# Scores of two items visited together in a one-core attention and expert block

## The chip, the cores and the metric

The kernel runs on one core of one Trainium2 chip. The metric is the device time of one execution in microseconds (us). TensorE is PE in the profile, its weight loads PEld, VectorE DVE, ScalarE ACT, GpSimd POOL, and SyncE (which issues the DMAs) SP.

## What is computed

For 16 batches of 512 rows with 256 channels: a layer norm, 16 heads of causal attention with RMS norm and rotary embedding on q and k, and beside it a layer of 8 experts of which each row takes one. Both are added to the input. Cut to what matters:

```python
xn = _layernorm(x)
q, k, v = split(einsum('btc,oc->bto', xn, wqkv))      # 16 heads of 64
q, k = rope(rmsnorm(q, q_norm_w)), rope(rmsnorm(k, k_norm_w))
attn = einsum('bhtd,bhsd->bhts', q, k) * D ** -0.5
attn = softmax(where(causal, attn, -inf))
out = einsum('bhts,bhsd->bhtd', attn, v) -> einsum('bte,ce->btc', out, wo)
chosen = argmax(einsum('bsh,eh->bse', xn, gate_w)); moe = xn + (xn @ expert_w[chosen])
return x + out + moe
```

## The kernel before

The work is cut into 128 units, one for each pair of heads of each batch (16 batches by 8 pairs). Rows come in four tiles of 128. `ITEMS = (1, 3, 2, 0)` is the order in which the row tiles of a unit are scored: item 0 is row tile 1 with 256 columns of keys, item 1 is tile 3 with 512, item 2 is tile 2 with 384 and item 3 is tile 0 with 128. Exact f32 products are made from high and low parts of the operands, in three terms (`TERMS`).

Every engine runs its own list of steps, written out by hand in a function `unit(u)`; the lists meet only at semaphores, and on each engine a step that waits holds all that stands behind it. While unit u is scored, unit u-1 is finished and units u+1 and u+2 are begun. The steps that matter here, with the name of the function, are:

- `qkv(u, t)` on PE: 6 products of 384 columns for row tile t. ACT takes the squares and v (`take_qkv`), DVE the products with cosine and sine and the sums (`rope_products`, three instructions), POOL adds and scales them. `transpose_qk` turns q and k, ACT and DVE split them in high and low part (`take_qk`).
- `scores(u, k)` on PE: for item k six products, three terms for each of two heads. A head has 64 rows of q and k, so a product uses half of the array's rows (64*128 in the profile) and the two heads' products start as a pair. Then two products over all rows add the causal mask on the diagonal tile (ident_b, mask_b, bf16). Items write two score buffers in turn, `ps_s[n % 2]`; the visit waits until the softmax two items back is done (`s_prob`).
- `row_max(u, k)` on DVE takes the maxima, `softmax(u, k)` on ACT the exponentials and their sums, two heads each.
- `transpose_probs(u, k)` (pt0 to pt3) turns the probabilities, ACT takes them (`take_pt`). One unit later `values(u)` multiplies them with v.
- `invert_sums(u)` on DVE: a reciprocal and a copy to row_inv. PE turns row_inv (`transpose_inverse`), ACT takes it (`take_inverse`), DVE multiplies (`normalise_o`), ACT and DVE split the result (`take_o`).
- `project(u)`: 12 products with w_out; DVE adds them (`take_projection`, to acc).
- `transpose_xs`, `expert` (xs, ex): one tile of sorted rows and its expert in most units.

Some units of a batch have extra steps on DVE: `row_stats` (pair 4), `normalise_x` (pair 5), `start_rows` (pair 1), `choose` (pair 7); every second batch `take_rank` (after `ranks` on PE), `find_slots` and `add_experts`. Units 0 to 7 have `split_weights`.

All PE outputs other than scores go to four general banks `ps_g` in strict rotation. `uses(u)` lists the uses of a unit in PE's order; a use waits for the release of the use four before it (`bank`). Reordering PE's list therefore also changes who has to have released what.

## Time and profile before

| | us |
|---|---|
| median of 3 executions | 2225.2 (2224.34 to 2225.23) |
| profiled execution | 2226.1 |
| its span, first to last instruction | 2224.0 |
| PE busy | 2119.9 (95%) |
| DVE busy | 1664.7 (75%) |
| ACT busy | 1526.2 (69%) |
| POOL busy | 1335.0 (60%) |
| granted TensorE clock, mean | 0.991 |

A busy engine is one that has an instruction of the program running; a wait is idle time before an instruction, put down to the semaphore that ended it. Matmuls overlap: what one costs is the distance between starts, not its duration. The profile's chain of work that ended last lies on PE for 78% of the span.

### The profile page before, as it was taken

What the parts mean: (1) busy time and instruction counts of PE and PEld (TensorE: products, weight loads), DVE (VectorE), ACT (ScalarE), POOL (GpSimd) and SP (SyncE); (2) the same over time, 40 slices, a digit from 0 to 9 for tenths busy, and PEclk for the clock granted to TensorE, in tenths of its full rate; (3) what the DMA queues carried; (4) which work ended last, traced back from release to release, by engine and by line L of the source; (5) the groups of instructions that cost most, each with busy time, mean ns of one, the idle gap of its engine ahead of it and who ended that gap; (6) DMA issues with size and microseconds to landing.
All of it is one profiled execution on the core that took longest, in us unless ns stands there. A gap on an engine that the chain in (4) does not pass through costs nothing.

```text
span 2224.0 us, 46872 instructions
## 1 busy us (share of the span) xinstructions
PE 2119.9 (95%) x16008; PEld 1685.9 (76%) x16008; DVE 1664.7 (75%) x3788; ACT 1526.2 (69%) x4689; POOL 1335.0 (60%) x1957
## 2 busy tenths in 40 slices
PE   3989999999999999999999999999999999999994
PEld 3767778777878777877777777877777877777773
DVE  6878777777777777777777777777777777777762
ACT  2666777767777667777777767776777767767772
POOL 3556655576665666557665576556666576555652
PEclk9999999999999999999999999999999999999997
DMA  5210211111211212111221121211221111211234
GB/s 172 67 39 20 72 44 55 56 64 47 87 53 44 73 62 72 58 44 58 73 75 44 58 68 63 73 47 51 69 68 63 49 57 63 77 63 44 65 114 149
DMA packets 84235, 145.71 MB, mean 66 GB/s; under 512 B 9760, under 2 KB 62880, under 8 KB 83872
## 3 DMA queue, kind: packets, MB, share of 16 engines
q1 hardware_dynamic: 77856, 125.93, 17.7%
q0 software_dynamic: 6144, 16.79, 2.3%
q8 instruction: 130, 2.13, 0.4%
q14 instruction: 105, 0.86, 0.1%
HBM read 102.05 MB, written 40.63 MB: 64 GB/s over the span
## 4 chain that ended last, share of the span: by engine, by line
PE 78%; DVE 9%; POOL 4%; ACT 3%; issue 3%; DMA 1%; SPq 0%; POOLq 0%; DVEq 0%
PE ps_g L648 31%; PE ps_g L744 12%; PE ps_s L721 12%; PE ps_g L735 11%; PE ps_g L708 5%; PE ps_s L724 4%; PE ps_g L752 3%; DVE neg_max L940 1%; POOL y_back L497 1%; DVE qk_sin L926 1%; ACT prob L554 1%; POOL qk_rot L467 1%; PE ps_g L673 1%; DVE acc L903 1%; ACT prob_t L562 1%
## 5 line engine op out<-in xcount | busy, mean ns | idle before, releaser
L467 POOL TENSOR_TENSOR qk_rot<-qk_cos,qk_sin 128x128 f32<-128x128 f32 x1024 | 471.9, 483 | 720.1 <-DVE qk_sin L926 707.3
L648 PE MATMUL ps_g<-w_qkv,xn_t 128*128 128x384 f32 (+1 forms) x3072 | 612.1, 348 | 20.1 <-DVE xn_t L841 14.9
L554 ACT ACTIVATE prob<-ps_s,neg_max 128x256 f32<-128x256 f32 (+3 forms) x1024 | 535.5, 537 | 114.2 <-DVE neg_max L940 114.2
L648 PEld LDWEIGHTS ps_g<-w_qkv,xn_t 128*128 128x128 f32 x3072 | 528.3, 190 | 32.9 <-issue 15.2
L940 DVE TENSOR_REDUCE neg_max<-ps_s 128x2 f32<-128x512 f32 (+3 forms) x512 | 417.4, 820 | 100.5 <-PE ps_s L724 92.6
L540 ACT ACTIVATE qk_sq<-ps_g 128x256 f32<-128x256 f32 x512 | 197.1, 385 | 367.4 <-PE ps_g L648 367.4
L562 ACT ACTIVATE prob_t<-ps_g 128x512 f32<-128x512 f32 (+2 forms) x768 | 378.5, 532 | 78.7 <-PE ps_g L735 72.0
L473 POOL TENSOR_TENSOR rms_inv<-ss,neg_half 128x8 f32<-128x8 f32 x256 | 422.5, 1650 | 0.0
L735 PE MATMUL ps_g<-ident,prob 128*128 128x128 f32 x2560 | 374.5, 276 | 5.7 <-ACT prob L554 2.7
L721 PE MATMUL ps_s<-k_t,q_t 64*128 64x256 f32 (+3 forms) x3072 | 373.9, 348 | 1.4 <-DVE q_t L934 1.4
L478 POOL TENSOR_TENSOR qk_rot<-qk_rot,rms_inv 128x256 f32<-128x256 f32 x512 | 310.9, 628 | 20.1
L721 PEld LDWEIGHTS ps_s<-k_t,q_t 64*128 64x128 f32 x3072 | 228.0, 185 | 113.5 <-issue 101.4
L735 PEld LDWEIGHTS ps_g<-ident,prob 128*128 128x128 f32 x2560 | 285.9, 141 | 35.8 <-issue 20.9
L744 PE MATMUL ps_g<-prob_t,v 128*64 128x512 f32 (+3 forms) x2048 | 303.9, 439 | 0.0
L926 DVE TENSOR_TENSOR qk_cos<-ps_g,t_cos 128x256 f32<-128x256 f32 x512 | 216.0, 422 | 75.2 <-ACT v L543 59.9
L744 PEld LDWEIGHTS ps_g<-prob_t,v 128*64 128x64 f32 x2048 | 135.6, 136 | 158.9 <-issue 140.4
L554 ACT ACTIVATION_READ_ACCUMULATOR prob<-ps_s,neg_max 128x1 f32 x1024 | 219.8, 215 | 0.0
L926 DVE TENSOR_TENSOR qk_sin<-ps_g,t_sin 128x256 f32<-128x256 f32 x512 | 212.1, 414 | 0.0
L929 DVE TENSOR_REDUCE ss<-qk_sq 128x4 f32<-128x260 f32 x512 | 211.7, 413 | 0.0
L648 PE MATMUL ps_g<-w_out,o_t 128*128 128x256 f32 x1536 | 204.2, 282 | 0.4 <-ACT prob_t L562 0.4
L648 PEld LDWEIGHTS ps_g<-w_out,o_t 128*128 128x128 f32 x1536 | 191.1, 189 | 0.6 <-issue 0.6
L966 DVE TENSOR_TENSOR acc<-ps_g,acc 128x512 f32<-128x512 f32 x128 | 88.3, 690 | 130.8 <-PE ps_g L648 130.8
(96 smaller groups left out, 2336.9 us busy)
## 6 DMA issues: line engine op xcount, KB each, us to landing
w_tile<-w_dram SPq DMA_DIRECT2D x120, 512.0 KB, 3.5
x_rows_s<-x_dram SPq DMA_DIRECT2D x120, 128.0 KB, 2.1
y_dram<-y_rows_s SPq DMA_DIRECT2D x120, 128.0 KB
xin<-in_x SPq DMA_DIRECT2D x16, 512.0 KB, 4.0
out<-acc SPq DMA_DIRECT2D x16, 512.0 KB, 3.0
w_dram<-w_tile SPq DMA_DIRECT2D x8, 512.0 KB, 3.0
x_dram<-xn SPq DMA_DIRECT2D x2, 1920.0 KB, 14.6
y_back<-in_expert_t SPq DMA_DIRECT2D x8, 256.0 KB, 4.1
```

The source lines that it names most:

```text
L467: r = pool.tensor_tensor(rot[:, :, a, :], cos[:, :, a, :], sin[:, :, 1 - a, :], ALU.add)
L473: pool.tensor_tensor(rms_inv[:, ts[0]:ts[-1] + 1, :], ss[:, ts[0]:ts[-1] + 1, :], neg_half[:, :, :], ALU.pow).then_inc(s_pool_self, 1)
L478: r = pool.tensor_tensor(rot, rot, rms_inv[:, t, :].unsqueeze(2).to_broadcast([P, 4, D]), ALU.mult)
L554: r = act.activation(prob[:, n % 2, h, 0:w], ps_s[n % 2][:, h, 0:w], ACT.Exp, bias=neg_max[:, i, h:h + 1], scale=1.0, accum_out=row_sum[:, ...
L562: act.activation(prob_t[:, h0:h1, 0:i + 1, tile(i)], ps_g[g_bank(u, f"pt{k}.{part}")][:, 0:(h1 - h0) * w].rearrange("p (h j q) -> p h j q" ...
L648: r = pe.matmul(ps, lhs(a, c), rhs(b, c), start=(c == parts[0] and (a, b) == TERMS[0]), stop=(c == parts[-1] and (a, b) == TERMS[-1]))
L721: pe.matmul(ps_s[n % 2][:, h, 0:w], q_t[rows, a, tile(i)], k_t[rows, b, 0:w], start=(m == 0), stop=(m == 2))
L735: r = pe.transpose(ps[:, tile((h - h0) * (ITEMS[k] + 1) + j)], prob[:, n % 2, h, tile(j)], ident[:, :])
L744: r = pe.matmul(ps[rows, j * P:], v[:, u % 3, j, rows], prob_t[:, h, j, j * P:], start=(j == 0), stop=(j == NT - 1), skip_group_check=True)
L926: r = dve.tensor_tensor(dst[:, t % 2, :].rearrange("p (n h d) -> p n h d", n=2, h=2), src, table[:, t, :, :].unsqueeze(2).to_broadcast([P, ...
L929: dve.tensor_reduce(ss[:, t, :], qk_sq[:, t % 2, :, :], AX.X, ALU.add).then_inc(s_sums, 1)
L940: dve.tensor_reduce(neg_max[:, i, :], ps_s[(NT * u + k) % 2][:, :, 0:w], AX.X, ALU.max, negate=True).then_inc(s_max, 1)
```

## The change

In `scores`, one visit now makes two items: first four mask products, two for each score buffer, as the first term of the sums (`start=True`), then the six products of the first item, then the six of the second, which add to what is there. The visit waits for the softmax of the item just before it, so for both buffers. A unit has two visits where it had four.

The lists move: on PE both first items stand before `qkv(u+1, 3)` at the head of the unit, pt0 and pt1 stand together, `transpose_xs` goes before the second visit, and pt3 goes between qkv tiles 1 and 2. On DVE `row_max(u, 0)` heads the unit, ahead of `invert_sums(u-1)`, `row_max(u, 1)` and `rope_products(u+1, 3)`; `take_xs` goes ahead of `row_max(u, 2)`; `normalise_x`, `row_stats`, `split_weights` stand ahead of `row_max(u, 3)`. On ACT softmax 0 and 1 stand around `take_qkv(u+1, 3)`, ahead of `take_inverse`.

```diff
--- before.py
+++ after.py
@@ -296,10 +296,8 @@
             if live(u - 1):
                 found += ["inv", "o"]
             if live(u):
-                found += ["pt0.0"]
+                found += ["pt0.0", "pt1.0", "pt1.1"]
             found += [f"xs{i}" for i in tiles[0:2]]
-            if live(u):
-                found += ["pt1.0", "pt1.1"]
             if turns_x(u):
                 found += ["xt0", "xt1"]
             found += [f"ex{i}" for i in tiles[0:1]] + [f"xs{i}" for i in tiles[2:3]] + [f"ex{i}" for i in tiles[1:3]]
@@ -311,10 +309,12 @@
                 found += ["kt", "qt"]
             if ranks_in(u) is not None:
                 found += ["rank"]
+            if live(u + 2):
+                found += ["qkv0", "qkv1"]
             if live(u):
                 found += ["pt3.0"]
             if live(u + 2):
-                found += ["qkv0", "qkv1", "qkv2"]
+                found += ["qkv2"]
             return tuple(found)
 
         @lru_cache(None)
@@ -589,22 +589,23 @@
 
             def unit(u):
                 tiles = sorted_tiles(u)
+                if live(u):
+                    softmax(u, 0)
                 if live(u + 1):
                     take_qkv(u + 1, 3)
                 if live(u):
-                    softmax(u, 0)
+                    softmax(u, 1)
                 if live(u - 1):
                     take_inverse(u - 1)
                 if live(u):
-                    softmax(u, 1)
                     take_pt(u, 0)
                 for i in tiles[0:2]:
                     take_xs(u, i)
                 if live(u - 1):
                     take_o(u - 1)
                 if live(u):
+                    take_pt(u, 1)
                     softmax(u, 2)
-                    take_pt(u, 1)
                 if turns_x(u):
                     take_xt(batch_of(u) + 1)
                 for i in tiles[0:1]:
@@ -708,22 +709,27 @@
                         r = pe.transpose(ps[:, tile(t)], qk_rot[:, t, tile(1 - n)], ident[:, :])
                     r.then_inc(s_qk_t, 1)
 
-            def scores(u, k):
-                i, w, n = ITEMS[k], width(k), NT * u + k
-                if k == 0:
+            def scores(u, k0):
+
+                n0 = NT * u + k0
+                if k0 == 0:
                     pe.wait_ge(s_qk_lo, 2 * (u + 1))
-                if n >= 2:
-
-                    pe.wait_ge(s_prob, 2 * (n - 1))
-                for m, (a, b) in enumerate(TERMS):
+                if n0 >= 2:
+
+                    pe.wait_ge(s_prob, 2 * n0)
+                for n in (n0, n0 + 1):
+                    i = ITEMS[n - NT * u]
                     for h in range(HEADS_OF_PAIR):
-                        rows = slice(h * D, (h + 1) * D)
-                        pe.matmul(ps_s[n % 2][:, h, 0:w], q_t[rows, a, tile(i)], k_t[rows, b, 0:w],
-                                  start=(m == 0), stop=(m == 2))
-                for h in range(HEADS_OF_PAIR):
-                    r = pe.matmul(ps_s[n % 2][:, h, tile(i)], ident_b[:, :], mask_b[:, :], start=False, stop=True,
+                        pe.matmul(ps_s[n % 2][:, h, tile(i)], ident_b[:, :], mask_b[:, :], start=True, stop=False,
                                   skip_group_check=True)
-                r.then_inc(s_scores, 1)
+                for n in (n0, n0 + 1):
+                    i, w = ITEMS[n - NT * u], width(n - NT * u)
+                    for m, (a, b) in enumerate(TERMS):
+                        for h in range(HEADS_OF_PAIR):
+                            rows = slice(h * D, (h + 1) * D)
+                            r = pe.matmul(ps_s[n % 2][:, h, 0:w], q_t[rows, a, tile(i)], k_t[rows, b, 0:w],
+                                          start=False, stop=(m == 2), skip_group_check=True)
+                    r.then_inc(s_scores, 1)
 
             def transpose_probs(u, k):
                 n = NT * u + k
@@ -755,24 +761,22 @@
 
             def unit(u):
                 tiles = sorted_tiles(u)
+                if live(u):
+                    scores(u, 0)
                 if live(u + 1):
                     qkv(u + 1, 3)
-                if live(u):
-                    scores(u, 1)
                 if live(u - 1):
                     transpose_inverse(u - 1)
                     values(u - 1)
                 if live(u):
                     transpose_probs(u, 0)
-                    scores(u, 2)
+                    transpose_probs(u, 1)
                 for i in tiles[0:2]:
                     transpose_xs(u, i)
                 if live(u):
-                    transpose_probs(u, 1)
+                    scores(u, 2)
                 if turns_x(u):
                     transpose_xn(batch_of(u) + 1)
-                if live(u):
-                    scores(u, 3)
                 for i in tiles[0:1]:
                     expert(u, i)
                 for i in tiles[2:3]:
@@ -787,14 +791,13 @@
                     transpose_qk(u + 1)
                 if ranks_in(u) is not None:
                     ranks(u)
-                if live(u):
-                    transpose_probs(u, 3)
                 if live(u + 2):
                     qkv(u + 2, 0)
                     qkv(u + 2, 1)
+                if live(u):
+                    transpose_probs(u, 3)
+                if live(u + 2):
                     qkv(u + 2, 2)
-                if live(u + 1):
-                    scores(u + 1, 0)
 
             pe.wait_ge(s_masks_pe, 1)
             transpose_xn(0)
@@ -969,35 +972,39 @@
             def unit(u):
                 tiles = sorted_tiles(u)
                 if live(u):
+                    row_max(u, 0)
+                if live(u - 1):
+                    invert_sums(u - 1)
+                if live(u):
                     row_max(u, 1)
+                if live(u + 1):
+                    rope_products(u + 1, 3)
                 if live(u) and pair_of(u) == START_PAIR:
                     start_rows(batch_of(u))
-                if live(u + 1):
-                    rope_products(u + 1, 3)
                 if live(u + 1) and pair_of(u) == CHOOSE_PAIR:
                     choose(batch_of(u) + 1)
                 if live(u - 1):
                     normalise_o(u - 1)
-                if live(u):
-                    row_max(u, 2)
                 for i in tiles[0:2]:
                     take_xs(u, i)
+                if live(u):
+                    row_max(u, 2)
                 if live(u - 1):
                     take_o(u - 1)
+                if live(u) and batch_of(u) + 1 < B and pair_of(u) == NORM_PAIR:
+                    normalise_x(batch_of(u) + 1)
                 if live(u) and batch_of(u) + 1 < B and pair_of(u) == STATS_PAIR:
                     row_stats(batch_of(u) + 1)
+                for i in tiles[2:3]:
+                    take_xs(u, i)
+                if 0 <= u < E:
+                    split_weights(u)
                 if live(u):
                     row_max(u, 3)
+                if slots_in(u) is not None:
+                    find_slots(slots_in(u))
                 if turns_x(u):
                     take_xt(batch_of(u) + 1)
-                if live(u) and batch_of(u) + 1 < B and pair_of(u) == NORM_PAIR:
-                    normalise_x(batch_of(u) + 1)
-                if 0 <= u < E:
-                    split_weights(u)
-                if slots_in(u) is not None:
-                    find_slots(slots_in(u))
-                for i in tiles[2:3]:
-                    take_xs(u, i)
                 if projection(u):
                     take_projection(u)
                 if ranks_in(u) is not None:
@@ -1011,10 +1018,6 @@
                     add_experts(added_in(u))
                 if live(u + 2):
                     rope_products(u + 2, 2)
-                if live(u):
-                    invert_sums(u)
-                if live(u + 1):
-                    row_max(u + 1, 0)
 
             dve.wait_ge(s_consts_dve, 64)
             row_stats(0)
```

PE in a plain unit, before, from the head of the unit (qkv tile 3 is the second row) to the expert; ps_s is a score buffer, ps_g a general bank:

```order
L721 MATMUL ps_s<-k_t,q_t 128x512 x6
L724 MATMUL ps_s<-mask_b,ident_b 128x128 x2
L752 MATMUL ps_g<-ident,row_inv 128x128 x4
L744 MATMUL ps_g<-prob_t,v 64x512 x2
L744 MATMUL ps_g<-prob_t,v 64x384 x2
L744 MATMUL ps_g<-prob_t,v 64x256 x2
L744 MATMUL ps_g<-prob_t,v 64x128 x2
L735 MATMUL ps_g<-ident,prob 128x128 x4
L721 MATMUL ps_s<-k_t,q_t 128x384 x6
L724 MATMUL ps_s<-mask_b,ident_b 128x128 x2
L673 MATMUL ps_g<-ident,x_rows_s 128x128 x2
L735 MATMUL ps_g<-ident,prob 128x128 x8
```

PE in the same place of the changed kernel:

```order
L723 MATMUL ps_s<-mask_b,ident_b 128x128 x4
L730 MATMUL ps_s<-k_t,q_t 128x256 x6
L730 MATMUL ps_s<-k_t,q_t 128x512 x6
L649 MATMUL ps_g<-w_qkv,xn_t 128x384 x6
L758 MATMUL ps_g<-ident,row_inv 128x128 x4
```

The two mask pairs and both items now head the unit, qkv tile 3 follows. Behind `values`, PE of the changed kernel goes on with pt0 and pt1 in one row:

```order
L741 MATMUL ps_g<-ident,prob 128x128 x12
L674 MATMUL ps_g<-ident,x_rows_s 128x128 x2
L723 MATMUL ps_s<-mask_b,ident_b 128x128 x4
L730 MATMUL ps_s<-k_t,q_t 128x384 x6
L730 MATMUL ps_s<-k_t,q_t 128x128 x6
L649 MATMUL ps_g<-w_tile,x_cols_s 128x256 x6
```

The masks went ahead of the scores in fours, and the scores of item 2 went behind pt1 and xs.

DVE in a unit with row statistics, before, from the reciprocal on:

```order
L944 RECIPROCAL sum_inv<-row_sum 128x8
L945 COPY row_inv<-sum_inv 128x512
L940 TENSOR_REDUCE neg_max<-ps_s 128x2 x2
L926 TENSOR_TENSOR qk_cos<-ps_g,t_cos 128x256
L926 TENSOR_TENSOR qk_sin<-ps_g,t_sin 128x256
L929 TENSOR_REDUCE ss<-qk_sq 128x4
L951 TENSOR_TENSOR o_n<-ps_g,inv_t 128x512
L940 TENSOR_REDUCE neg_max<-ps_s 128x2
L895 TENSOR_TENSOR x_cols_s<-ps_g,x_cols_s 128x256
L955 TENSOR_TENSOR o_t<-o_n,o_t 128x512
L819 BN_STATS ln_stat<-xin 128x6 x4
```

And the same in the changed kernel, one row earlier:

```order
L943 TENSOR_REDUCE neg_max<-ps_s 128x2
L947 RECIPROCAL sum_inv<-row_sum 128x8
L948 COPY row_inv<-sum_inv 128x512
L943 TENSOR_REDUCE neg_max<-ps_s 128x2
L929 TENSOR_TENSOR qk_cos<-ps_g,t_cos 128x256
L929 TENSOR_TENSOR qk_sin<-ps_g,t_sin 128x256
L932 TENSOR_REDUCE ss<-qk_sq 128x4
L954 TENSOR_TENSOR o_n<-ps_g,inv_t 128x512
L898 TENSOR_TENSOR x_cols_s<-ps_g,x_cols_s 128x256
L943 TENSOR_REDUCE neg_max<-ps_s 128x2
L958 TENSOR_TENSOR o_t<-o_n,o_t 128x512
L822 BN_STATS ln_stat<-xin 128x6 x4
```

The maximum of item 0 went ahead of the reciprocal, and the maximum of item 2 behind x_cols_s.

## Rows read from the trace of the kernel before

**Rows 1.** stretches: us, busy PE, PEld, DVE, ACT, POOL, clock, DMA share, GB/s

```profile
344.61:360.76 16.15, 16.15 (x125) 13.02 (x125) 11.53 (x25) 11.76 (x37) 9.01 (x15) 1.00 0.16 50
376.92:393.71 16.79, 16.73 (x126) 12.99 (x125) 13.32 (x34) 11.77 (x37) 10.19 (x16) 1.00 0.15 49
393.71:409.85 16.14, 16.14 (x126) 13.00 (x125) 12.83 (x29) 11.76 (x37) 8.86 (x15) 1.00 0.16 50
```

**Rows 2.** waits of PE: engine, line, waited for, us in total, times, longest

```profile
PE ps_g L752 <- DVE row_inv L945: 10.7, 27, 0.6
```

**Rows 3.** timeline of PE, plain unit: start us, us, engine, line, operation, count

```profile
344.88 0.62 PE L721 MATMUL ps_s<-k_t,q_t 64*128 64x256 f32 x6
...
345.53 1.30 PE L648 MATMUL ps_g<-w_qkv,xn_t 128*128 128x384 f32 x6
346.76 0.96 PE L721 MATMUL ps_s<-k_t,q_t 64*128 64x512 f32 x6
...
347.78 0.61 PE L752 MATMUL ps_g<-ident,row_inv 128*128 128x128 f32 x4
...
350.62 0.66 PE L735 MATMUL ps_g<-ident,prob 128*128 128x128 f32 x4
351.21 0.79 PE L721 MATMUL ps_s<-k_t,q_t 64*128 64x384 f32 x6
...
352.05 0.39 PE L673 MATMUL ps_g<-ident,x_rows_s 128*128 128x128 f32 x2
352.28 1.04 PE L735 MATMUL ps_g<-ident,prob 128*128 128x128 f32 x8
353.25 0.55 PE L721 MATMUL ps_s<-k_t,q_t 64*128 64x128 f32 x6
...
353.82 0.96 PE L648 MATMUL ps_g<-w_tile,x_cols_s 128*128 128x256 f32 x6
```

**Rows 4.** timeline of PE, second and third pair of the scores of item 2

```profile
351.49 0.34 PE L721 MATMUL ps_s<-k_t,q_t 64*128 64x384 f32 x2
...
351.66 0.34 PE L721 MATMUL ps_s<-k_t,q_t 64*128 64x384 f32 x2
```

**Rows 5.** timeline of PE near the end: masks followed by scores

```profile
2167.29 0.28 PE L724 MATMUL ps_s<-mask_b,ident_b 128*128 128x128 bf16 x2
2167.51 0.73 PE L721 MATMUL ps_s<-k_t,q_t 64*128 64x512 f32 x4
```

**Rows 6.** timeline of DVE in the plain unit

```profile
346.58 0.19 DVE L944 RECIPROCAL sum_inv<-row_sum 128x8 f32<-128x8 f32 x1
346.81 0.43 DVE L945 COPY row_inv<-sum_inv 128x512 f32<-128x512 f32 x1
...
352.25 0.96 DVE L940 TENSOR_REDUCE neg_max<-ps_s 128x2 f32<-128x768 f32 x1 [0.75 <-PE ps_s L724]
```

**Rows 7.** timeline of DVE and PE where the inverse's transposes waited

```profile
481.51 0.43 DVE L945 COPY row_inv<-sum_inv 128x512 f32<-128x512 f32 x1
481.85 1.81 DVE L940 TENSOR_REDUCE neg_max<-ps_s 128x2 f32<-128x512 f32 x2
...
481.99 0.33 PE L752 MATMUL ps_g<-ident,row_inv 128*128 128x128 f32 x1 [0.18 <-DVE row_inv L945]
```

**Rows 8.** timeline of DVE: the extra work of four units

```profile
386.46 1.39 DVE L819 BATCH_NORM_STATS2 ln_stat<-xin 128x6 f32<-128x256 f32 x4
...
403.56 1.37 DVE L834 TENSOR_SCALAR xn<-xin,ln_mv,ln_rstd 128x256 f32<-128x256 f32 x4
...
474.04 0.69 DVE L966 TENSOR_TENSOR acc<-ps_g,acc 128x512 f32<-128x512 f32 x1
...
612.18 1.37 DVE L903 TENSOR_TENSOR acc<-acc,y_back 128x1024 f32<-128x1024 f32 x1
```

**Rows 9.** timeline of PE in a unit with ranks

```profile
458.04 3.25 PE L648 MATMUL ps_g<-w_qkv,xn_t 128*128 128x384 f32 x17 [0.65 <-DVE k_t L934]
```

**Rows 10.** groups of instructions by shape, ACT: busy us, mean ns of one

```profile
L554 ACT ACTIVATE prob<-ps_s,neg_max 128x384 f32<-128x384 f32 x256 | 145.8, 577 | 15.6 <-DVE neg_max L940 15.6
```

More of the change, by code:

```diff
@@ L789, in unit @@
                     ranks(u)
+                if live(u + 2):
+                    qkv(u + 2, 0)
+                    qkv(u + 2, 1)
                 if live(u):
@@ L792, in unit @@
                 if live(u + 2):
-                    qkv(u + 2, 0)
-                    qkv(u + 2, 1)
                     qkv(u + 2, 2)
-                if live(u + 1):
-                    scores(u + 1, 0)
             pe.wait_ge(s_masks_pe, 1)
```

4 lines of the change are left out of this document (2 added, 2 removed).

## The prediction

> **Forecast: the kernel becomes slower, about 2256 us, by 1.4%.** The change takes array switches off TensorE (PE) that are really there, but puts work of VectorE (DVE) ahead of two things that PE waits for.
>
> **What bounds the kernel now.** I first read busy time in stretches, cut at the last product of qkv for tile 2, which I call the origin of a unit. A plain unit lasts 16.15 us with PE busy for all of it, against 11.53 on DVE and 11.76 on ScalarE (ACT); units with extra DVE work last 16.14 (normalise) and 16.79 (statistics) [rows 1]. Then the waits: in all 128 units the inverse's transposes waited on DVE only 27 times, 10.7 us together [rows 2]. So PE's own instructions set the pace, and the others have slack. The question is how large each slack is, since the change spends it.
>
> **What PE saves.** Times below are from the origin of one plain unit, 344.61 [rows 1], and its instructions [rows 3]. Ordinary transposes run at a pace of 0.11 us (two in 352.05 to 352.28). The eight of pt1 and the step to the scores take 0.97 (352.28 to 353.25), so the step into two half arrays costs some 0.10 extra; then the first pair takes 0.28 where the next takes 0.17 [rows 4], another 0.11: 0.21 per entry. By the same rows the step out of the halves costs some 0.09 extra, and masks behind the scores put their own switch there. The changed unit has two entries and two exits less.
>
> Second half of the unit, pt0 to expert. Before: 350.62 to 353.82, 3.20 us. After: four pt0 0.50 (0.59 less the extra step), eight pt1 0.87, two xs 0.23, four masks and the entry 0.34, three pairs of item 2 0.62 (0.28 + 0.17 + 0.17), three of item 3 0.42 (0.11 + 0.11 + exit 0.20): 2.98. The unknown is masks ahead of scores. The one place where this stands in the trace, near the end, gives 0.22 for two masks with the entry [rows 5], two more at 0.06 give 0.34. If masks ran at the pace of transposes the sum would be 0.10 more; if they hid their weight loads, 0.05 less. **Saved: 0.23 us**, 0.13 to 0.28.
>
> The Trainium skill's "TensorEngine Tiling (Array Packing)", Key Properties, says that changing the tiling mode drains the engine; the rows agree (0.20 where 0.11 is the pace). With the warm latency in "TensorE: Matmul & The Clock Gate", Single matmul latency, (398+N)/2.4 ns, an estimate of a full entry and exit is 0.33 us instead of my 0.23; over 128 units that estimate would give 13 us less than my sum.
>
> First half. Before, the inverse's transposes start at 3.17 (347.78). After: to the masks 0.18, masks and entry 0.34, item 0 0.35 (344.88 to 345.53 is 0.65, less exit and masks 0.30), 0.12 to item 1, its pairs and exit 0.79 (346.76 to 347.78 is 1.02, less first-pair extra 0.11 and masks 0.12), six qkv 0.98 (1.23 less the entry, plus an exposed weight load), 0.18: PE arrives at 2.94, so 0.23 earlier.
>
> **What takes the place of the first saving.** The transposes need row_inv. DVE starts the reciprocal at 1.97 (346.58) and ends the copy at 2.63 [rows 6]; this slack of 0.54 hides it today. What comes ahead of the reciprocal follows qkv tile 2 through ACT, so it keeps its distance from the origin. The change puts row_max(u,0) ahead of it. That maximum is 0.61 (two maxima take 1.81 [rows 7], of which the wide one is 1.2). Ready: 1.97 + 0.61 + 0.66 = 3.24. Where PE did wait, it started 0.05 after the copy's end (481.94 to 481.99 [rows 7]): 3.29 instead of 2.94. **A new wait of 0.35 us in nearly every unit.** A waited start also finds no weights loaded, 0.06 more. So the first half ends 0.18 later than before, the second saves 0.23: -0.05 to -0.07, I take **-0.07 us a unit, -9 us** in all (-17 to +4). The queue behind the reciprocal on DVE (row_max(u,1), rope products 3) starts no later than before, and softmax 0 and 1 on ACT end some 0.5 us before pt1.
>
> The pt3 transposes that move between qkv 1 and 2 cost PE nothing: same steps, another order. The scores' wait on both pairs of banks is met long before, since pt1 needs the same probabilities; price 0. Banks in another rotation: normalised o is needed 0.3 us after it is ready in a plain unit; 0.
>
> **What is late in the units with extra DVE work.** Scores 2 move behind pt1 and xs. Before, row_max(u,2) starts at 7.64 (352.25) [rows 6], 1.04 after the group. After, PE starts that group at 6.01 + 0.18 + 0.50 + 0.87 + 0.23 + 0.34 = 8.13, and without masks behind it the maximum can start 0.83 later, at 8.96. It is 1.3 later; take_xs now stands ahead of it and not behind (0.34). So DVE is through take_o **0.97 us later**. In a plain unit this hides (projection needs DVE only at 11.5). Where extra work follows it does not, because row_max(u,3) and take_projection stand behind it, and q's transposes wait for the bank of the projection:
> - Statistics, 15 units. Their 1.91 us (386.46 and what follows [rows 8]) begin 0.97 later; take_projection ends at 13.45, PE wants the bank at 12.45. With the following wait for pt2's bank the unit is 1.29 over a plain one, before 0.64 [rows 1]. +0.65 each, **+9.7**.
> - Normalising, 15 units: 1.3 us (403.56 [rows 8]) moves ahead of row_max(u,3). Before nothing over a plain unit [rows 1], after take_projection ends at 12.83 and softmax 3 with pt2 is late: +0.67, **+10.0**.
> - Finding the slots, 8 units: take_projection starts 0.97 later than today's 474.04 [rows 8], where PE already waits: +1.05, **+8.4**.
> - Splitting the weights, units 3 to 6, which wait on take_projection too: +0.9, **+3.6**.
> - Units where DVE reaches the reciprocal late, 28 of them: half behind add_experts (1.37, 612.18 [rows 8]), half behind GpSimd, as at 481.99. There 0.54 of slack hid part of the lateness, now none: +0.45 and +0.23, **+9.5**.
> - Choosing experts, 15 units: its block stands ahead of normalise_o, whose bank xs now needs sooner. No row isolates it; between 0 and the 0.65 of the statistics, I take 0.25: **+3.8**.
> - Ranks, 8 units: PE waited 0.65 for k_t at qkv 0 [rows 9]; in the new rotation that bank goes to qkv 1, one tile later: -0.9 with the smaller waits around it, **-7.3**.
> - Units without a tile: softmax 2 is late for pt2 by 0.5, which replaces other small waits: **+1.9**.
>
> Sum: -9.0 + 9.7 + 10.0 + 8.4 + 3.6 + 9.5 + 3.8 - 7.3 + 1.9 = +30.6. Against the profiled span 2224.0 that is 2254.6; the medians lie 1.2 above the span: **2256 us**.
>
> **Rivals.**
> 1. The waits do not appear and PE keeps all it saves: about 0.47 us a unit. For it: PE is busy all through a plain unit, and the switches are in the rows. Against: 1.97 is fixed by qkv 2 through ACT. It decides at the copy's end: if row_inv is ready before 2.9, the base is -0.47 x 128 = -60 and the time 2165; with the special units' costs still there, 2165 + 40 = 2205. Chance 0.12.
> 2. The terms cancel: the switch is dearer than my rows (0.33) and the special units inherit less: -13 and half of the +37: about 2225. Chance 0.08.
> 3. Slower still: a second wait in every plain unit. Softmax 2 now starts when row_max(u,2) ends, 9.92, and takes about 1.2 (two of 0.58 and the last accumulator read [rows 10]), so pt2's transposes at 11.35 have 0.2 us left. If the maximum came 0.3 us later than I have it, each unit loses 0.1 to 0.2: +13 to +26, so 2269 to 2282. Chance 0.10.
> That the change does not group the work is excluded: the order shows four masks and then twelve products in a row.
>
> **How the numbers follow.** Forecast 0.70 (2236 to 2275 with its bounds), rivals 0.12, 0.08, 0.10. Rival 1 is left out of the range, the others are in: 2224 to 2282. A measurement can tell 0.2% (4.5 us) from no change. Slower by more than that: 0.70 + 0.10, and a little less for the forecast's low edge; same: most of rival 2, 0.07; faster: rival 1 and an edge, 0.14.
>
> **What would show it.** In the new profile: PE waits <- DVE row_inv in over 100 units, 0.3 us each; a plain unit of 16.1; row_max(u,2) starting near 9.0 after the origin; statistics units at 17.4; PE busy time per unit lower by 0.4. Wrong would be: no row_inv waits, or plain units below 15.9.

## The result and the profile after

The changed kernel takes 2265.9 us (median of 4 runs, 2265.1 to 2267.3) against 2225.2 before: ratio 1.018, 95% interval 1.017 to 1.020. The forecast was 2256 with a range of 2224 to 2282. The profiled execution of the changed kernel is 2263.7 us from first to last instruction, 39.7 more than before's 2224.0; the sum had given 30.6.

Of the page after: the span, the busy time of each engine, and the shares of the chain that ended last.

```profile
span 2263.7 us, 46872 instructions
...
PE 2087.3 (92%) x16008; PEld 1718.2 (76%) x16008; DVE 1643.7 (73%) x3788; ACT 1531.7 (68%) x4689; POOL 1352.7 (60%) x1957
...
PE 57%; DVE 26%; ACT 6%; POOL 5%; issue 5%; DMA 1%; SPq 0%; POOLq 0%; DVEq 0%
```

PE has less to do than before and yet the kernel is longer; on the chain, DVE has risen from 9% to 26%. The stretches of a plain unit, a statistics unit, and a normalise unit (columns as in [rows 1]):

```profile
356.34:372.35 16.01, 15.82 (x125) 13.19 (x125) 11.46 (x25) 11.76 (x36) 9.22 (x15) 1.00 0.15 50
388.37:405.66 17.29, 16.29 (x125) 13.22 (x125) 13.04 (x34) 11.87 (x36) 10.14 (x15) 1.00 0.15 47
405.66:422.33 16.67, 16.30 (x126) 13.22 (x125) 12.51 (x29) 11.88 (x36) 9.22 (x15) 1.00 0.16 50
```

The plain unit is down from 16.15 to 16.01, with 0.19 us in which PE idles. Statistics went from 16.79 to 17.29, normalise from 16.14 to 16.67. PE's waits by what ended them (us in total, times, longest), where [rows 2] had 10.7 us in 27 waits:

```profile
PE ps_g L758 <- DVE row_inv L948: 49.8, 128, 1.4
PE ps_g L709 <- DVE acc L969: 36.6, 40, 2.6
```

So the inverse's transposes now wait for row_inv in every one of 128 units. The second row is q's transposes, waiting for the bank of the projection; before that row was:

```profile
PE ps_g L708 <- DVE acc L966: 15.6, 13, 2.5
```

PE and then DVE in a plain unit with its origin at 356.34 (start, length, engine, line, operation), which answer to [rows 3] and [rows 6]:

```profile
356.52 0.40 PE L723 MATMUL ps_s<-mask_b,ident_b 128*128 128x128 bf16 x4
356.85 1.32 PE L730 MATMUL ps_s<-k_t,q_t 64*128 64x256 f32 x12
...
359.60 0.66 PE L758 MATMUL ps_g<-ident,row_inv 128*128 128x128 f32 x4 [0.19 <-DVE row_inv L948]
360.19 2.37 PE L750 MATMUL ps_g<-prob_t,v 128*64 128x512 f32 x16
362.49 1.53 PE L741 MATMUL ps_g<-ident,prob 128*128 128x128 f32 x12
...
364.08 0.39 PE L723 MATMUL ps_s<-mask_b,ident_b 128*128 128x128 bf16 x4
364.39 1.07 PE L730 MATMUL ps_s<-k_t,q_t 64*128 64x384 f32 x12
365.40 0.86 PE L649 MATMUL ps_g<-w_tile,x_cols_s 128*128 128x256 f32 x5
```

```profile
358.30 0.68 DVE L943 TENSOR_REDUCE neg_max<-ps_s 128x2 f32<-128x512 f32 x1
358.90 0.19 DVE L947 RECIPROCAL sum_inv<-row_sum 128x8 f32<-128x8 f32 x1
359.12 0.43 DVE L948 COPY row_inv<-sum_inv 128x512 f32<-128x512 f32 x1
...
365.23 0.96 DVE L943 TENSOR_REDUCE neg_max<-ps_s 128x2 f32<-128x768 f32 x1
```

The reciprocal starts 2.56 after the origin, which is the last product of qkv tile 2 (before: 1.97), behind the row maximum at 1.96; the copy ends at 3.21 and PE starts at 3.26 with 0.19 us of waiting. The maximum of item 2 starts at 8.89 (7.64 before).

### The profile page after: what moved, and what is told of

Same layout as the page of the kernel before. It is cut to its first block, busy times and chain, and to the rows that moved or that the text cites. A ratio compares the mean times of both kernels' runs of the same rounds, so it can differ in the third digit from the quotient of the medians.

```text
span 2263.7 us, 46872 instructions
## 1 busy us (share of the span) xinstructions
PE 2087.3 (92%) x16008; PEld 1718.2 (76%) x16008; DVE 1643.7 (73%) x3788; ACT 1531.7 (68%) x4689; POOL 1352.7 (60%) x1957
## 3 DMA queue, kind: packets, MB, share of 16 engines
q0 software_dynamic: 6144, 16.79, 2.3%
## 4 chain that ended last, share of the span: by engine, by line
PE 57%; DVE 26%; ACT 6%; POOL 5%; issue 5%; DMA 1%; SPq 0%; POOLq 0%; DVEq 0%
PE ps_g L649 22%; PE ps_g L750 11%; PE ps_g L741 10%; DVE neg_max L943 7%; PE ps_s L730 4%; PE ps_g L709 4%; PE ps_g L758 3%; DVE qk_sin L929 3%; DVE qk_cos L929 3%; DVE ss L932 2%; DVE row_inv L948 2%; ACT prob L554 2%; ACT qk_sq L540 2%; PE ps_g L674 1%; POOL qk_rot L467 1%
## 5 line engine op out<-in xcount | busy, mean ns | idle before, releaser
L649 PE MATMUL ps_g<-w_qkv,xn_t 128*128 128x384 f32 (+1 forms) x3072 | 646.2, 354 | 17.6 <-DVE xn_t L844 14.8
L473 POOL TENSOR_TENSOR rms_inv<-ss,neg_half 128x8 f32<-128x8 f32 x256 | 448.3, 1751 | 0.0
L741 PE MATMUL ps_g<-ident,prob 128*128 128x128 f32 x2560 | 353.8, 276 | 17.4 <-ACT prob L554 13.9
L478 POOL TENSOR_TENSOR qk_rot<-qk_rot,rms_inv 128x256 f32<-128x256 f32 x512 | 304.2, 615 | 20.1
L730 PE MATMUL ps_s<-k_t,q_t 64*128 64x256 f32 (+3 forms) x3072 | 306.6, 331 | 0.0
L554 ACT ACTIVATION_READ_ACCUMULATOR prob<-ps_s,neg_max 128x1 f32 x1024 | 205.4, 201 | 0.0
L937 DVE TENSOR_TENSOR k_t<-ps_g,k_t 128x512 fp32r<-128x512 f32 x128 | 88.3, 690 | 152.3 <-ACT k_t L548 152.3
## 6 DMA issues: line engine op xcount, KB each, us to landing
x_dram<-xn SPq DMA_DIRECT2D x2, 1920.0 KB, 14.8
```

The source lines that it names most:

```text
L473: pool.tensor_tensor(rms_inv[:, ts[0]:ts[-1] + 1, :], ss[:, ts[0]:ts[-1] + 1, :], neg_half[:, :, :], ALU.pow).then_inc(s_pool_self, 1)
L478: r = pool.tensor_tensor(rot, rot, rms_inv[:, t, :].unsqueeze(2).to_broadcast([P, 4, D]), ALU.mult)
L554: r = act.activation(prob[:, n % 2, h, 0:w], ps_s[n % 2][:, h, 0:w], ACT.Exp, bias=neg_max[:, i, h:h + 1], scale=1.0, accum_out=row_sum[:, ...
L649: r = pe.matmul(ps, lhs(a, c), rhs(b, c), start=(c == parts[0] and (a, b) == TERMS[0]), stop=(c == parts[-1] and (a, b) == TERMS[-1]))
L730: r = pe.matmul(ps_s[n % 2][:, h, 0:w], q_t[rows, a, tile(i)], k_t[rows, b, 0:w], start=False, stop=(m == 2), skip_group_check=True)
L741: r = pe.transpose(ps[:, tile((h - h0) * (ITEMS[k] + 1) + j)], prob[:, n % 2, h, tile(j)], ident[:, :])
```

## The experiments

Ratios are always to the kernel before, run beside each kernel on the same chip. On the chip of e1, e2, e3 and e5 it takes 2243.4 us, beside all others 2225.2 to 2225.9; so across these two groups ratios are compared, not microseconds. That chip shows a second peculiarity. In units 9 to 122 the profiles of e1, e2, e3 and e5 hold waits of DVE and ACT of more than 0.3 us for which the profile names no semaphore of the program (it puts them down as issue or remote), 22 to 34 us together in each; the other nine profiles, all from where it takes 2225, hold none. The expectations were written as times where the kernel before takes 2225, so for these four the ratio times 2225.2 is what compares with them.

### What do pairing and the masks' place each give?

e4: the masks first, visits still one by one, in the kernel before.

```diff
 def scores(u, k):
+    for h in range(HEADS_OF_PAIR):
+        pe.matmul(ps_s[n % 2][:, h, tile(i)], ident_b[:, :], mask_b[:, :], start=True, stop=False, ...)
     for m, (a, b) in enumerate(TERMS):
...
-                      start=(m == 0), stop=(m == 2))
-    for h in range(HEADS_OF_PAIR):
-        r = pe.matmul(... ident_b[:, :], mask_b[:, :], start=False, stop=True, ...)
+                      start=False, stop=(m == 2), skip_group_check=True)
```

> The kernel before, four visits as before, with the two mask products ahead of the six score products in each visit (as the first term of the sum) and nothing else. It tells whether the gain on PE is from masks ahead of scores or from two items per visit. Theory (only the number of entries to and exits from the half arrays counts, and it is unchanged; with masks ahead, the exposed weight load behind the exit falls on a larger f32 product and not on a bf16 mask): +0 to +0.2 us a unit, 2225 to 2250. Rival (masks ahead are what saves): 2170 to 2210.

Measured 2237.9, ratio 1.0056 [1.004, 1.007]. e7: the changed kernel, two items side by side, but the four masks behind the twelve products.

```diff
 def scores(u, k0):
-    for n in (n0, n0 + 1): (the two masks of n, start=True)
     for n in (n0, n0 + 1): (the six products of n; now the first starts the sum)
+    for n in (n0, n0 + 1): (the two masks of n, stop=True)
         r.then_inc(s_scores, 1)
```

> The changed kernel with the four masks behind the twelve score products of a visit. Switches are as few as in the changed kernel; the first item's scores are complete some 1 us later in each visit. Theory (the pairing saves, not the masks' place; row_max(u,0) still has time, row_max(u,2) starts 0.3 later or more and eats the 0.2 us that softmax 2 has left before pt2, and pushes DVE's extra work later): 2275 to 2300. Rival (the masks' place is worth nothing at all): 2262 to 2270.

Measured 2298.6, ratio 1.033 [1.031, 1.034]. A plain unit of e4 and one of e7:

```profile
343.98:360.29 16.31, 16.31 (x126) 13.25 (x125) 11.52 (x25) 11.76 (x37) 8.99 (x15) 1.00 0.16 49
```

```profile
363.21:379.45 16.24, 15.97 (x125) 13.12 (x125) 11.41 (x25) 11.76 (x36) 9.24 (x15) 1.00 0.16 49
```

The four arrangements of a plain unit: single with masks last 16.15 (before), single with masks first 16.31 (e4), paired with masks last 16.24 (e7), paired with masks first 16.01 (after). Masks first costs 0.16 where visits stand alone and gains 0.23 where they are paired. In e4 PE is busy for the whole 16.31, so this is the price on PE itself. In e7 PE reaches the expert as early as in the changed kernel, 9.05 after the origin against 9.06. But the maximum of item 2 starts at 9.17 against 8.89, because it has to wait for the masks at the end, and pt2's transposes start at 11.45 against 11.28. So paired visits gain by masks ahead because the maximum can start sooner, not on PE. This is rival 3 of the prediction, made on purpose: 0.3 later costs 0.2 in each unit and, with the units that have extra steps, 1.4% in all. Both times lie in the ranges expected.

### Is the new wait the late reciprocal?

e3 gives the kernel before only that order; e1 takes it out of the changed kernel; e2 puts the inversion earlier still, between products 1 and 2 of the preceding unit.

```diff
     rope_products(u + 2, 2)     # e3, kernel before
-    invert_sums(u)
     row_max(u + 1, 0)
+    invert_sums(u)
...
-    row_max(u, 0)               # e1, changed kernel
     invert_sums(u - 1)
+    row_max(u, 0)
     row_max(u, 1)
...
     row_max(u, 0)               # e2, changed kernel
-    invert_sums(u - 1)
     row_max(u, 1)
...
     rope_products(u + 2, 1)
+    invert_sums(u)
     add_experts(added_in(u))
     rope_products(u + 2, 2)
```

> The kernel before with this alone: row_max(u+1,0) ahead of invert_sums(u) on DVE. Nothing else of the change. Theory: the slack of 0.54 us of the reciprocal is less than the maximum's 0.61, a wait of 0.12 plus 0.06 in plain units and the full 0.61 in the 28 units where DVE is late: +30 to +40 us, 2255 to 2265. Rival (PE has more slack there than read, or the order at the head does not matter): 2222 to 2232.

Measured 2260.0, ratio 1.0074 [1.006, 1.009]. Its plain unit is 16.31, as expected, and the units already late rise by 0.6:

```profile
346.57:362.88 16.31, 16.31 (x125) 13.06 (x125) 11.45 (x25) 11.88 (x37) 9.06 (x15) 1.00 0.15 49
616.92:634.45 17.53, 16.36 (x125) 13.05 (x125) 12.58 (x26) 11.88 (x37) 10.25 (x15) 1.00 0.23 76
```

The unit lengths of its profile add up to 32 us over those of before's profile, and its span is 34.1 longer; but that profile is from another chip, and on e3's own chip the difference of the times is 16.6 us. The kernel before itself takes 18.2 us more on this chip, and 34.1 less 18.2 is 15.9. In which units the 18.2 would stand no run shows. So the swap costs 17 us, about half of the 30 to 40 that were expected: the time of 2260.0 lies in the expected range only because of the chip, and the ratio gives 2242, above the rival's 2232 and under the theory's 2255.

> The changed kernel with one thing undone on DVE: invert_sums(u-1) stands ahead of row_max(u,0) again, at the head of the unit. Theory (the new wait of PE for row_inv, 0.35 us in each unit, comes from the 0.61 us maximum ahead of the reciprocal): the row_inv waits fall from 49.8 us to below 12; but row_max(u,0) and with it softmax 0, qkv 3, softmax 1 and the inverse on ACT end 0.6 us later against PE, so that the xs transposes now wait some 0.3 us for o_n; a plain unit goes from 16.02 to about 15.9 and the kernel to 2245 to 2256. Rival (the order at the head is all there is): plain unit 15.6, 2205 to 2220. Rival (the maximum is not the cause): 2260 or more, row_inv waits stay.

Measured 2286.9, ratio 1.0198 [1.018, 1.022], which is 2269 where the kernel before takes 2225, above the 2245 to 2256 expected: no gain on the changed kernel, though PE's waits for row_inv fell from 49.8 us to 17.6.

> The changed kernel with the reciprocal and the copy to row_inv moved further ahead, between the rope products of tiles 1 and 2 of unit u+2, where DVE is idle for some 0.2 us. row_max(u,0) then starts only 0.36 us later than in the changed kernel. Theory: neither row_inv nor o_n is late any more, PE keeps what the pairing of the scores saves, plain unit 15.6 to 15.7, kernel 2205 to 2225, at or below the kernel before. Rival (pairing saves PE nothing, the plain unit is 16.0 for another reason): 2255 or more.

Measured 2261.3, ratio 1.0081 [1.006, 1.010], which is 2243 by the same reckoning, 1.0% under the changed kernel and over the 2225 expected. The plain units did what was expected, 15.91 (e1) and 15.66 (e2), and the totals did not follow. In e2 the first row is the plain unit and the second the unit with added experts and choose, 17.72 in the changed kernel:

```profile
351.89:367.55 15.66, 15.66 (x125) 13.24 (x125) 11.47 (x25) 11.64 (x36) 9.27 (x15) 1.00 0.17 51
569.75:590.10 20.35, 16.60 (x125) 13.26 (x125) 14.56 (x44) 11.78 (x38) 14.10 (x19) 1.00 0.32 93
```

Six units of this kind take 20.30 to 20.42. In this one the inversion and the added experts (1.4 us) both stand ahead of products 2, so the two maxima start at 3.72, 0.7 later than in the changed kernel; choose stands behind them, normalise_o ends at 9.72, and PE, which comes earlier now, waits 1.4 for it, after 0.9 for the late softmax 1. In e1 the same units went from 17.7 to between 19.8 and 20.3. Over the whole of e2, PE's waits for the normalised output rose from 6.0 us in 14 waits to

```profile
PE ps_g L674 <- DVE o_n L954: 25.2, 47, 1.4
```

PE's other 1.5 us of waiting in this unit are odd. They go with late starts of ACT and DVE, of which this is the first:

```profile
586.23 0.87 ACT L562 ACTIVATE prob_t<-ps_g 128x384 f32<-128x384 f32 x2 [2.03 <-remote]
```

The last of pt2's transposes had ended at 584.23, yet ACT took the bank at 586.23, and DVE took the projection 1.2 us after PE was through with it. In this stretch DMA is busiest of the whole unit (share 0.70, GpSimd's gathers and the expert's weights), and one packet of the queue that the page calls q8, instruction, ran from 584.88 to 586.29. Whether ACT waited for code behind that traffic no run settles; packets of this queue of up to 2.2 us stand in profiles without such waits too (b0). The same wait of ACT stands in units of this kind in e1 and e2 (2.0 to 2.1 us) and e5 (1.6), three different edits on the chip where the kernel before takes 2243, and in no profile of another chip. That speaks for the chip and not for the edit. In e2's units 79 and 111 ACT does not wait like this; there 20.4 us come about by a stretch of half clock instead.

So the theory "the reciprocal is the new wait" holds for the plain unit (0.16 in e3, 0.10 in e1, 0.35 in e2). As an account of the total it fell: much of what was won in a plain unit was lost in the special ones. How much of that loss is the edit's and how much the chip's is open, since neither e1 nor e2 ran on another chip.

### Can the extra steps just go last?

e5 moves row_stats, normalise_x and split_weights behind take_projection in the changed kernel; e6 moves find_slots there.

```diff
-   normalise_x(...), row_stats(...), split_weights(u)      (e5)
    row_max(u, 3)
-   find_slots(slots_in(u))                                 (e6)
    take_xt(...), take_projection(u)
+   the moved ones
```

> The changed kernel with normalise_x, row_stats and split_weights moved behind take_projection on DVE. Theory (they delay row_max 3 and take_projection, which cost +0.65 and +0.67 us in 15 units each): normalise units fall from 16.67 to 16.1, statistics units from 17.3 to about 16.4 (a late reciprocal stays), the first units by some us in all; the kernel 2238 to 2250. Rival (the wait only moves on to k_t and q_t, which now stand behind): 2260 to 2270.

Measured 2278.7, ratio 1.016 [1.014, 1.018]: no better than the changed kernel's 1.018 within the intervals, where 2238 to 2250 had been expected (the ratio gives 2261).

> The changed kernel with find_slots (3.1 us, 8 units) behind take_projection and not ahead of it. Theory: the 2.06 us wait of q's transposes in those units goes, and with it the stretches at half clock that follow it in some of them; k_t, q_t and the scatter on GpSimd become late by 1.3 us instead and show up as a wait of 1 to 2 us there and for row_inv one unit later: 2255 to 2268, little or nothing gained. Rival (nothing is behind it): the 8 units fall from 18.3 and 19.8 to 16.1, 2240 to 2246.

Measured 2287.3, ratio 1.028 [1.026, 1.030], 19 us over the highest value expected. In e5 the statistics unit fell from 17.29 to 16.33 and the normalise unit from 16.67 to 16.02. But unit 29 rose from 17.88 to 22.85 (five more like it to between 21.3 and 22.7). GpSimd just ahead of it and in it, PE's wait, and the stretch after that wait:

```profile
529.70 1.01 POOL L460 TENSOR_TENSOR ln_rstd<-ln_ve,neg_half 128x4 f32<-128x4 f32 x1 [5.15 <-DVE ln_ve L827]
530.88 1.06 POOL L497 DMA_INDIRECT y_back<-y_dram,slot_i  x1 [0.18 <-issue]
...
533.51 0.95 POOL L497 DMA_INDIRECT y_back<-y_dram,slot_i  x1 [0.30 <-issue]
534.76 0.94 POOL L497 DMA_INDIRECT y_back<-y_dram,slot_i  x1 [0.30 <-issue]
535.72 1.68 POOL L467 TENSOR_TENSOR qk_rot<-qk_cos,qk_sin 128x128 f32<-128x128 f32 x4
```

```profile
539.00 1.12 PE L758 MATMUL ps_g<-ident,row_inv 128*128 128x128 f32 x4 [4.10 <-DVE row_inv L948]
540.05 4.54 PE L750 MATMUL ps_g<-prob_t,v 128*64 128x512 f32 x16
```

```profile
539.00:544.58 5.58, 5.58 (x21) 2.51 (x22) 2.07 (x4) 2.81 (x9) 5.42 (x10) 0.50 0.00 0
```

The late statistics hold back GpSimd's ln_rstd (5.15 us of waiting), the four gathers stand behind it, 1.25 to 1.37 us apart, and the rotations behind those, until 535.72; products 2 on DVE wait for a buffer of the rotations, the reciprocal stands behind the products, and PE waits 4.10 us. After that the granted clock is 0.50, 1.2 GHz, and the 16 values take 4.54 us where they take 2.37 in a plain unit. In e6 it is the scatters that start later, and the same chain follows: unit 26, behind one with slots, goes from 16.88 to 20.67 with a wait of 3.15 us (the longest of its kind is 3.4), while unit 25, which finds the slots, fell from 18.29 to 17.39.

### VectorE's steps in the gaps that its rows show

Two waits of DVE in the plain unit of the changed kernel, behind normalise_o and between take_projection and take_qk:

```profile
364.70 0.42 DVE L898 TENSOR_TENSOR x_cols_s<-ps_g,x_cols_s 128x256 fp32r<-128x256 f32 x1 [1.32 <-ACT x_cols_s L580]
...
369.71 0.69 DVE L937 TENSOR_TENSOR k_t<-ps_g,k_t 128x512 fp32r<-128x512 f32 x1 [1.20 <-ACT k_t L548]
```

e8 keeps the inversion of e2. The row statistics go one unit earlier, where GpSimd has neither scatters nor gathers, and nearly every extra step goes into one of these two gaps, in two parts where it is longer than the gap; the rest of find_slots stays behind row_max 3. e9 is the same with the inversion where the change has it. e10 gives the extra steps these places in the kernel before.

```diff
-STATS_PAIR = 4
+STATS_PAIR = 3
 def unit(u):      # of VectorE
     normalise_o(u - 1)
+    start_rows (ahead of it in a unit with slots), first 4 steps of find_slots,
+    max and max_index of choose, bn_stats of 3 tiles
     take_xs, row_max(u, 2), take_o(u - 1), row_max(u, 3)
+    rest of find_slots
     take_xt, take_projection(u)
+    rest of row_stats, normalise_x, rest of choose, split_weights(u), add_experts
     take_rank, take_qk(u + 1), rope_products(u + 2, 0), rope_products(u + 2, 1)
+    invert_sums(u)            (e8 alone)
     rope_products(u + 2, 2)
```

> The changed kernel with the inversion early (as in the run e2: between products 1 and 2 of the unit before) and, beside it, VectorE's extra steps moved into the gaps that its own rows show: the row statistics one unit earlier (pair 3, where GpSimd scatters and gathers nothing) and in two parts (three tiles behind the normalised output, the rest behind the taken projection); choose and find_slots in two parts each; start_rows behind the normalised output; the normalised x, the split weights and the added experts behind the taken projection. Theory A (the units of the change lost time because steps of VectorE stood on the way of a value that TensorE waited for, and nothing else): a plain unit 15.66 us as in e2, the statistics, normalise and choose units within 0.4 us of it, the unit with added experts and choose 16.2 to 16.6 where e2 took 20.35; by the sum over the units 2258 - 19 - 10 - 10 - 4 - 28 - 8 - 9 - 9 = 2161, and with half of that lost again 2210; ratio to the kernel before 0.965 to 0.985. Rival B (paired score visits lose to TensorE itself, masks and the shorter lead between a score visit and its softmax): not under 1.0, whatever VectorE does.

> As e8, but the inversion where the change has it, behind the first row maximum of the next unit. Theory A: a plain unit is 16.02 as in the changed kernel, so e9 is slower than e8 by 0.36 us in some 100 units, 30 to 45 us, and still under the kernel before on its chip: ratio 0.98 to 1.0. Rival: the late reciprocal costs nothing once the extra steps are out of the way, e9 within 10 us of e8.

> The kernel before (single score visits) with the same extra steps of VectorE moved into its gaps; products, inversion and row maxima stand where the kernel before has them. Its units above the plain 16.15 in the profile of before: statistics 0.63 x15, choose 0.3 x16, added experts 1.3 x8, slots 1.2 x8, unit 13 0.46 x8, first units about 8; together some 45 us, of which half to all comes back: ratio 0.98 to 0.99, a plain unit still 16.15. Against e8 it tells what the paired score visits are worth with everything else in place: theory A gives e8 the lead by about 0.4 us in each unit (15.7 against 16.15, 40 to 60 us); rival B gives e10 the lead.

> The kernel before, unchanged, for its profile on this chip beside e8 to e10: ratio 1.000 within 0.2%. If this chip is one on which it takes 2243 us and not 2225, the profile shows where the 18 us are: stretches at half the granted clock (then a few units are about 2 us longer and the rest as before), or slower transfers (then the waits for the landing of expert weights), or every unit longer by 0.8%.

The four runs and the changed kernel, all where the kernel before takes 2225:

| kernel | score visits | inversion | extra steps | us | ratio, 95% |
|---|---|---|---|---|---|
| b0 | single | before's | before's | 2225.0 | 1.000 [0.999, 1.001] |
| e10 | single | before's | in gaps | 2204.6 | 0.990 [0.988, 0.992] |
| e9 | paired | the change's | in gaps | 2192.9 | 0.985 [0.983, 0.987] |
| e8 | paired | early | in gaps | 2150.8 | 0.966 [0.964, 0.968] |
| changed kernel | paired | the change's | the change's | 2265.9 | 1.018 [1.017, 1.020] |

The ratios and plain units of all four came out as expected. By its time e8 did better than the 2161 of the sum, and e10 got back 20 us of some 45, a little under the half that was expected. e8 beats both kernels: 3.4% under before, 5.1% under the change (2150.8 / 2265.9). From e8's page, then its plain unit, its normalise unit, and the unit that took 20.35 in e2:

```profile
span 2148.3 us, 46895 instructions
...
PE 2049.6 (95%) x16008; PEld 1719.5 (80%) x16008; DVE 1656.5 (77%) x3788; ACT 1513.9 (70%) x4689; POOL 1338.5 (62%) x1957
...
PE 82%; DVE 9%; ACT 4%; issue 3%; POOL 1%; DMA 1%; SPq 0%; POOLq 0%; DVEq 0%
```

```profile
340.46:356.13 15.67, 15.67 (x125) 13.26 (x125) 11.47 (x25) 11.64 (x36) 9.24 (x15) 1.00 0.16 52
387.47:403.13 15.66, 15.66 (x126) 13.24 (x125) 12.66 (x29) 11.64 (x36) 9.25 (x15) 1.00 0.15 52
549.79:565.57 15.78, 15.78 (x125) 13.26 (x125) 13.55 (x43) 11.78 (x38) 13.23 (x20) 1.00 0.28 81
```

One unit does not fit. Unit 11 takes 18.36 in e8, 19.13 in e9 and 20.32 in e10, where the changed kernel has 15.75 and before 15.60: the statistics, moved one unit earlier, there wait 2.4 to 3.4 us for the load of x to land.

PE waits on row_inv once in the whole of e8 (first row), in e9 still in all 128 units (second):

```profile
PE ps_g L758 <- DVE row_inv L954: 0.5, 1, 0.5
```

```profile
PE ps_g L758 <- DVE row_inv L954: 33.2, 128, 1.2
```

The extra steps in the gaps are worth 20.4 us to the kernel before (b0 to e10), but 73 to the changed one (to e9), some 6 of them from four stretches of half clock (below). So it was the change that made these steps dear. With them in gaps, the change gives 11.7 us (e10 to e9) even with the late reciprocal, and the early inversion 42.1 more (e9 to e8). The 11.7 are for the paired visits together with the list moves that came with them; no run parts the two.

## Why the prediction was right, term by term

Direction and mechanism were right, and the time is inside the range; the sum came out 9.1 us low against the spans. That it is as near as this is in part luck: by the table below some terms were too high by 10.4 us together and others too low by 19.5. The terms, measured by the lengths of units (sums over the units named; from units 9 to 122 each has the plain unit's shift of 0.13 taken out):

| term | forecast, us | measured, us |
|---|---|---|
| plain unit's shift, units 9 to 122 | -8.0 | -14.8 |
| statistics, 14 units | +9.1 | +9.1 |
| normalise, 14 units | +9.4 | +9.2 |
| late reciprocal | +9.5 | +6.1 |
| choose, 14 units | +3.5 | +5.7 |
| slots, with the unit behind | +8.4 | +15.0 |
| ranks, 7 units | -6.4 | -5.8 |
| no tile | +1.9 | +1.9 |
| units with x transposed and others | 0 | +1.8 |
| units 1 to 8 | +3.7 | +6.1 |
| start, unit 0, units from 123 on, drain | -0.5 | +5.4 |
| sum | +30.6 | +39.7 |

- **The saving on PE.** pt0 to expert took 2.91 us (from 362.49 to 365.40) where the sum had 2.98 and before 3.20. Four masks and the entry are 0.31 (364.08 to 364.39) against 0.34, from rows of two masks near the end [rows 5]. (The sum's own terms give 3.20 less 2.98, so 0.22 and not 0.23 was forecast.) This and the start of the inverse's transposes at 3.26, not 3.29, are where the plain unit did better than forecast. "TensorEngine Tiling (Array Packing)" of the Trainium skill, Key Properties, says that a change of tiling mode drains the engine. These runs agree in sign, since pairing leaves fewer changes and PE's busy time is 15.82 instead of 16.15 in a plain unit.
- **The new wait.** Forecast 3.29 for the start of the inverse's transposes, measured 3.26, in 128 of 128 units. e3 and e1 show its cause from both sides. Rival 1 (no wait) is thereby excluded here; with the wait gone and nothing else late, as in e8, the plain unit is 15.67, which is the -0.47 that this rival gave each unit, nearly to the digit.
- **Item 2's maximum.** Forecast 8.96, measured 8.89. The mechanism of rival 3 exists, as e7 shows, but the changed kernel stays 0.3 us clear of it. Rival 2 fell: the special units did inherit the whole lateness.
- **Statistics, normalise, ranks, no tile.** Within 0.6 us of the sum. That take_projection is late by what DVE is late, and that nothing cushions it, was read off rightly: these four terms give +14.4 measured against +14.0.
- **The term that was mis-sized: slots.** +1.05 a unit was forecast. Four of eight units have +0.94 over before, or 1.07 with the plain shift. The other four (units 9, 41, 73, 105) have 2.5 over before. Their PE waits 2.06 us for the projection just as in the others (2.33 in unit 9), but then the twelve products of qkv run mostly at half clock: the mean over them is 0.56 of full speed, between the levels 0.50 (1.2 GHz) and 1.00 (2.4 GHz). First the stretch of such a unit, of one without, and of the twelve products alone; then PE in both:

```profile
744.03:763.86 19.83, 17.58 (x125) 14.70 (x125) 15.23 (x39) 11.87 (x36) 14.43 (x19) 0.91 0.18 57
472.97:491.26 18.29, 16.04 (x125) 13.18 (x125) 15.20 (x39) 11.87 (x36) 12.90 (x17) 1.00 0.16 52
759.04:762.93 3.89, 3.89 (x18) 3.85 (x16) 1.91 (x5) 1.15 (x3) 2.98 (x4) 0.56 0.29 101
```

```profile
758.63 0.66 PE L709 MATMUL ps_g<-ident,qk_rot 128*128 128x128 f32 x4 [2.06 <-DVE acc L969]
759.04 3.89 PE L649 MATMUL ps_g<-w_qkv,xn_t 128*128 128x384 f32 x12
...
487.56 0.66 PE L709 MATMUL ps_g<-ident,qk_rot 128*128 128x128 f32 x4 [2.06 <-DVE acc L969]
487.98 2.36 PE L649 MATMUL ps_g<-w_qkv,xn_t 128*128 128x384 f32 x12
```

3.89 against 2.36 us after the same wait. The prediction priced waits by their length alone, and no term held the clock that a wait can cost. Before's profile had the case once, and the profile of the same kernel in b0 has the same place without it. First before, then b0:

```profile
139.53 0.66 PE L708 MATMUL ps_g<-ident,qk_rot 128*128 128x128 f32 x4 [1.89 <-DVE acc L966]
...
140.16 4.94 PE L648 MATMUL ps_g<-w_qkv,xn_t 128*128 128x384 f32 x18
```

```profile
139.87 0.66 PE L708 MATMUL ps_g<-ident,qk_rot 128*128 128x128 f32 x4 [1.87 <-DVE acc L966]
...
140.50 3.40 PE L648 MATMUL ps_g<-w_qkv,xn_t 128*128 128x384 f32 x18
```

So the same wait of the same kernel cost 1.5 us more in one execution than in another. "TensorE: Matmul & The Clock Gate" of the Trainium skill, Part 1, says that the granted clock follows how busy PE has recently been. This case agrees in kind: behind a wait of 2.06 us the clock fell in units 41, 73 and 105 (759.04 to 762.93: 0.56 granted) and stayed at 1.00 in units 25, 57, 89 and 121. What decides between the two no run shows.
- **The start.** Units 0, 1 and 2 came out 2.2, 1.7 and 1.3 us longer, and no term held that. They have neither a tile nor a projection, so pt2's transposes follow the scores of item 2 at once, and nothing covers the later maximum and softmax of that item. In unit 1 PE waits 2.04 us, where before it waited 0.7:

```profile
74.04 0.87 PE L741 MATMUL ps_g<-ident,prob 128*128 128x128 f32 x6 [2.04 <-ACT prob L554]
```

The split weights ahead of row_max 3 add to it (1.25 us of waiting for ACT behind pt2 in unit 1), but they are not the main cause: in e5 they stand behind, the wait of 2.04 us is still there, and units 0 to 2 are 2.5 us longer in sum than in the changed kernel, partly at half clock. Unit 4 came out 3.2 longer, again with half clock, after a wait of 2.60 us. In units 3 to 8 e5 is 9.0 us shorter than the changed kernel; there the split weights count, as the forecast had it for units 3 to 6. (e5 ran on the chip of 2243, which may add to its lengths.)
- **Choose** was set at 0.25 from between 0 and 0.65 and is 0.41 on average.

What stays open: what the one chip does to take 2243 for the kernel before (b0 ran where it takes 2225, so there is no profile of that), whether the waits without a named semaphore in its profiles are the reason, and what these waits are; and what made the last units 3 us longer than before.

## To carry to other kernels

A change on the engine that sets the pace must be followed into the queue that feeds it: here 0.33 us of TensorE's busy time was saved in a plain unit, and the steps put ahead of two values on VectorE cost more. Extra steps that come once in some units went best into the gaps that the feeding engine's rows show, cut to the gap's length. One must also ask whose queue waits for their result, since e5 and e6 moved steps off one path and onto GpSimd's, and lost. Once the steps stood right, the same change that had cost 1.8% was part of a gain of 3.4%.

## What the chip showed that was not expected

- A wait of TensorE can cost more than itself: in four of eight like units, waits of 2.06 us (2.33 in one) were followed by twelve products mostly at half clock (0.56 granted on average), 1.5 us lost; 4.10 us of waiting (e5) was followed by half clock too, 2.2 us lost on the values alone.
- A gather through indices keeps GpSimd busy for 0.94 to 1.06 us, and four in a row start 1.25 to 1.37 us apart; everything queued behind them waits, as e5's rows show.
- Masks ahead of products cost a single visit 0.16 us per unit in PE's own time (e4, 16.31 for 16.15), though four visits hold the same instructions as before.
- The same kernel takes 0.8% longer on one chip than on the others (2243.4 against 2225.2), and only profiles from that chip hold waits of VectorE and ScalarE that the profile puts down to no semaphore (up to 2.1 us on ScalarE). Runs on different chips are compared by their ratios to a kernel that ran beside them.
